# A graph and attention layer on one core: every k product ahead of every q product in the projections, counts begun three products earlier, a denser track of edge maxima

## The chip, the cores and the metric

One core of a Trainium2 chip runs the whole program. A core has five engines, each with its own in-order stream of instructions: TensorE (PE; its weight loads are shown apart as PEld), VectorE (DVE), ScalarE (ACT), GpSimd (POOL) and SyncE (SP), which here only issues DMAs. They meet through semaphores. The metric is the time of one execution on the device in microseconds, and a lower one is better. A difference under about 0.3% (5 us here) can't be told from no change by these measurements.

## The reference, cut to what matters

`xn` is the layer norm of `x` (1250 nodes, 768 columns). Three branches follow.

```python
# graph: three layers of graph attention over 21250 edges (+ loops), 4 heads of 192
h = (x1 @ W).reshape(N, H, C)
e = leaky_relu(as_n[src] + ad_n[dst], 0.2)
m = segment_max(e, dst);  p = exp(e - m[dst]);  s = segment_sum(p, dst)
out = segment_sum((p / s[dst])[:, :, None] * h[src], dst)
# mix: linear attention with random features, 12 heads of 64, 256 features
dash = (d ** -0.25 * data) @ proj.T          # for q and for k
diag = sum(data * data) * 0.5 * d ** -0.5
q' = ratio * (exp(dash - diag - max over the features of the row) + EPS)
k' = ratio * (exp(dash - diag - max over ALL heads, rows, features) + EPS)
out = q' (k'^T v) / (q' sum k');  mix = out @ w_proj.T + b_proj
x = x + relu(concat(graph layers) @ W_out + b_out) + mix
x = x + switch_ffn(layer_norm(x))            # 8 experts, top 1, capacity 195
```

The maximum of the k features runs over all twelve heads. So no k feature can be formed before every k projection and its `dash` product exist. The q maximum is one per row.

## The kernel before, in words

The nodes lie in NT = 10 tiles of 128 rows (98 in the last). The graph is not gathered edge by edge: indirect DMAs on POOL (`place`, L2093) scatter-add the edges into three tables of 1250x1250 counts in DRAM. Each tile of them is read back (`tab_in`), added on DVE and cast on ACT (`count`), turned on PE (`count_turn`), and made into `absent` on DVE, 0 where there is an edge and -3e38 where there is none (L1440). With `absent` in place, `edge_max` (L1452) is one DVE instruction per head and tile that takes the maximum of `as + absent` over a row: 12 heads x 10 tiles = 120. After the 40 of a layer, `shifts` forms exp's shifts on DVE, turns them (L1474) and writes them to DRAM; `head_in` reads them back as broadcast rows (`shift_b`). Then come 120 items of attention, each half a head by two tiles: `edge_z` (DVE, L1489 twice), `edge_exp` (ACT, L1882 twice), `weigh` (DVE, L1498) and `gather` (PE, 20 matmuls of L1047 into banks 0 to 2). `evict` and `finish` empty a half head.

Beside it runs the mix. The projections are 2 x 6 blocks n of 128 columns (a pair of heads each), by three chunks c of rows (512, 512, 226): 36 products m = 3n + c. A product (`qk`, PE, 18 matmuls) is squared and scaled on ACT, split into high and low parts on DVE (`qk_split`, L1387), its norms are matmuls (`norms`, L993, then DVE L1397), and a finished block is stored (`qk_store`, L2197). For a k block, ten `k_top` steps (three 512-column matmuls on PE, and DVE L1405, 0.69 us) take the maximum of each tile. Before the change even blocks are k and odd blocks q of the same pair, and the `k_top` of a k block are laid between the products of the q block behind it. After the last product come `top_max`, `top_turn` and `top_spread`, which make the one maximum. Then per pair of heads: ten `dash` for k with `k_exp` and `k_sum`, ten `dash` for q with `q_exp` (DVE L1521 and L1526, ACT L1921), `q_turn`, `q_feat`, `q_out` (L1101) and `divide` (L1536), and three steps of drain: 23 steps. Last come the output products of three of the row blocks (`row_block`: `row_in`, `row_turn` L1116, `row_split`, `row_mm`, `row_add`); in them the weights of the next block are loaded and split (`out_load`, `out_split` L1541). `expert_setup` prepares the routing once the graph's rows are out: POOL waits for their DMA, writes tables of indices, and DVE converts them (L1584 to L1588).

What stands where is set by one list, `ORDER`, that every engine runs through and of which it executes its own part. `whole_order` weaves generators into it. A `None` ends a step. The projections and then the mix advance one step at a time; a product is two steps. The graph's track advances beside them by rates: a rate of 0.75 yields an `edge_max` in three steps of four. `done` carries marks from one track to the other: `scattered` lets the counts begin, `projected` ends the first track's first part, `edges` is set after the last `edge_max`. The steps are numbered through here: the projections are steps 70 to 143 in both kernels.

## Time and profile before

| | us |
|---|---|
| median of 3 runs | 1726.52 |
| lowest, highest | 1725.98, 1729.97 |
| the profiled execution | 1718.87 |
| its span, first to last instruction | 1717.1 |

The profiled execution is itself 7.65 us below the median, and 1.8 us of it lies outside the span. A difference worked out on the trace is therefore taken off the median, not the trace's own time. PE is busy 91% of the span, DVE 66%, ACT 40%. To read such a profile for this change, one goes from the shares by engine to the busy time in stretches, and there asks which engine another one waits for.

### The profile page before, as it was taken

The page shows a single profiled execution, that of the slowest core. Times are in us where ns is not written, and L with a number is a line of the kernel's source. Part 1 is how long each engine was busy: PE and PEld are TensorE (multiplying, and loading weights), DVE is VectorE, ACT ScalarE, POOL GpSimd, SP SyncE. Part 2 cuts the span into 40 slices and gives each one's busy share as a digit, 9 for nine tenths or more (in the row PEclk, how much of TensorE's full clock was granted, in tenths as well). Part 3 has the DMA queues.
Part 4 walks back from the last instruction along what each step waited for, and adds up shares of the span by engine and source line. Part 5 has one row for each costly group of instructions (what it writes and reads, how often), then busy time and mean ns, then how long its engine had stood idle before and what let it go on. Part 6 is the DMA issues. An engine that isn't in the chain of part 4 may idle for free.

```text
span 1717.1 us, 24932 instructions
## 1 busy us (share of the span) xinstructions
PE 1565.3 (91%) x9666; PEld 1192.4 (69%) x9731; DVE 1129.8 (66%) x2573; ACT 681.6 (40%) x1359; POOL 410.1 (24%) x251
## 2 busy tenths in 40 slices
PE   3979999999989789999999979999999999986987
PEld 2556666555655467888888868888888966656664
DVE  6677664114466978797878789767975643885223
ACT  3421001122233467777777754434643431441110
POOL 3788888888400000000000000000000000002331
PEclk9999999999999979999999999999999999996999
DMA  9335545454652223234233044334530133645941
GB/s 353 84 67 118 119 78 118 68 94 65 191 183 87 91 78 135 72 99 131 63 101 95 27 153 134 129 129 151 164 125 29 60 114 135 231 180 211 321 146 50
DMA packets 194504, 213.66 MB, mean 124 GB/s; under 512 B 80975, under 2 KB 149213, under 8 KB 194386
## 3 DMA queue, kind: packets, MB, share of 16 engines
q1 hardware_dynamic: 117762, 187.01, 33.0%
q0 software_dynamic: 75760, 22.70, 8.4%
q10 hardware_dynamic: 864, 2.36, 0.4%
q8 instruction: 77, 1.26, 0.3%
q14 instruction: 41, 0.34, 0.1%
HBM read 144.74 MB, written 68.40 MB: 124 GB/s over the span
## 4 chain that ended last, share of the span: by engine, by line
PE 72%; DVE 17%; ACT 4%; issue 3%; DMA 2%; SPq 1%; POOLq 0%; POOL 0%; ACTq 0%; DVEq 0%
PE bank L1047 19%; PE bank L892 12%; PE bank L893 12%; PE bank L891 12%; PE bank L1217 4%; DVE junk L1452 3%; PE bank L1205 3%; PE bank L1101 3%; PE bank L1073 2%; DVE eb L1498 1%; DVE eb L1489 1%; PE bank L1116 1%; DVE q_max L1521 1%; PE bank L1086 1%; PE bank L993 1%
## 5 line engine op out<-in xcount | busy, mean ns | idle before, releaser
L1047 PE MATMUL bank<-hb,eb 128*128 128x193 f32 (+3 forms) x2400 | 419.9, 332 | 24.7 <-DVE eb L1498 14.0
L1047 PEld LDWEIGHTS bank<-hb,eb 128*128 128x128 f32 (+3 forms) x2400 | 400.3, 190 | 38.3 <-DVE eb L1498 17.1
L2093 POOL DMA_INDIRECT table<-amount,place x170 | 345.1, 2030 | 71.5 <-issue 49.5
L2099 POOL IOTA iota8i<- 128x8 int32 x1 | 0.1, 139 | 934.6 <-DMA node_rows<-node 934.6
L1489 DVE SCALAR_TENSOR_TENSOR eb<-shift_b,as_low,shift_b 128x640 f32<-128x640 f32 (+1 forms) x240 | 196.3, 859 | 7.8 <-DMA shift_b<-shift_rows 7.8
L1882 ACT ACTIVATE eb<-eb,asd 128x640 f32<-128x640 f32 (+1 forms) x240 | 182.0, 814 | 45.9 <-DVE eb L1489 45.9
L1498 DVE SCALAR_TENSOR_TENSOR eb<-eb,count 128x1280 f32<-128x1280 f32 (+1 forms) x120 | 174.4, 1454 | 12.4 <-ACT eb L1882 12.4
L1452 DVE CUSTOM_DVE_ANT_0 junk<-ab,absent 128x1250 bf16<-128x1250 f32 x120 | 174.4, 1453 | 1.0
L891 PE MATMUL bank<-wg_hi,x1T_hi 128*128 128x384 bf16 (+3 forms) x360 | 117.9, 328 | 0.6 <-DVE x1T_lo L1319 0.6
L893 PE MATMUL bank<-wg_hi,x1T_lo 128*128 128x384 bf16 (+3 forms) x360 | 117.9, 327 | 0.0
L892 PE MATMUL bank<-wg_lo,x1T_hi 128*128 128x384 bf16 (+3 forms) x360 | 117.8, 327 | 0.0
L891 PE MATMUL bank<-w_o_hi,aT_hi 128*128 128x384 bf16 (+1 forms) x360 | 117.4, 326 | 0.0
L893 PE MATMUL bank<-w_o_hi,aT_lo 128*128 128x384 bf16 (+1 forms) x360 | 117.3, 326 | 0.0
L892 PE MATMUL bank<-w_o_lo,aT_hi 128*128 128x384 bf16 (+1 forms) x360 | 117.3, 326 | 0.0
L892 PE MATMUL bank<-xnT_lo,wq_hi 128*128 128x512 bf16 (+1 forms) x211 | 72.0, 341 | 3.4 <-DVE wq_lo L1295 2.8
L893 PE MATMUL bank<-xnT_hi,wq_lo 128*128 128x512 bf16 (+1 forms) x215 | 73.4, 341 | 0.3
L1754 DVE TENSOR_TENSOR orow<-bank,b2r 105x384 f32<-105x384 f32 (+1 forms) x32 | 17.8, 556 | 84.5 <-PE bank L1217 76.1
L1333 DVE TENSOR_TENSOR h_row<-bank,bgr 128x384 f32<-128x384 f32 (+1 forms) x60 | 32.5, 555 | 62.1 <-PE bank L893 58.8
L1921 ACT ACTIVATE ef<-bank,q_shift 128x256 f32<-128x256 f32 (+1 forms) x120 | 50.3, 472 | 56.9 <-DVE q_shift L1526 56.9
L891 PE MATMUL bank<-xnT_hi,wq_hi 128*128 128x512 bf16 (+1 forms) x207 | 70.2, 339 | 0.2
L1828 ACT ACTIVATE wg_hi<-stage 128x776 bf16<-128x776 f32 x18 | 15.3, 850 | 132.9 <-DVE stage L1309 118.6
L1921 ACT ACTIVATE ef<-bank,k_shift 128x256 f32<-128x256 f32 (+1 forms) x120 | 49.9, 468 | 37.9 <-PE bank L893 37.6
(288 smaller groups left out, 2944.1 us busy)
## 6 DMA issues: line engine op xcount, KB each, us to landing
w<-in_w SPq DMA_DIRECT2D x16, 1152.0 KB, 20.1
shift_b<-shift_rows SPq DMA_DIRECT2D x24, 625.0 KB, 5.9
h_rows<-h_row SPq DMA_DIRECT2D x27, 388.0 KB
hb<-h_rows SPq DMA_DIRECT2D x12, 873.0 KB
ar<-node_rows SPq DMA_DIRECT2D x27, 384.0 KB
table<-zero POOLq DMA_DIRECT2D x3, 3054.0 KB, 21.1
tab<-table SPq DMA_DIRECT2D x27, 312.5 KB, 3.4
qk_rows<-qk_row SPq DMA_DIRECT2D x12, 625.0 KB
```

Source lines behind the costliest of these rows:

```text
L891: T.matmul(out_ap, lhs[0], rhs[0], start=first, stop=False, skip_group_check=skip)
L892: T.matmul(out_ap, lhs[0], rhs[1], start=False, stop=False, skip_group_check=skip)
L893: return T.matmul(out_ap, lhs[1], rhs[0], start=False, stop=last, skip_group_check=skip)
L1047: ins = T.matmul(bank[w // 2][0:M, c0:c0 + GC + 1], p[0:K, u, w * P:w * P + M], hv[0:K, t, 0:GC + 1], start=opens and u == 0 and w % 2 == ...
L1101: ins = T.matmul(ov[0:R, u, hh, :], qf[q % 4][:, hh * MT + m, 0:R], context[:, m, hh, :], start=u == 0 and hh == 0 and m == 0, stop=m == M ...
L1217: ins = T.matmul(bank[4 + i % 4][0:r1 - r0, 0:HROWS], hT[e % 2][:, f, r0:r1], w2s[e % WEIGHT_SETS][:, f, cs], start=f == 0, stop=f == KF - 1)
L1452: V.tensor_tensor_reduce(out=junk[0:R, :], in0=ab[lh % 2][0:R, :], in1=absent[0:R, t, :], scale=1.0, scalar=-BIG, op0=ALU.add, op1=ALU.max ...
L1489: ins = V.scalar_tensor_tensor(eb[i % EDGE_BUFFERS][:, u, 0:w], low, as_low[:, t, lh:lh + 1], high, ALU.add, ALU.max)
L1498: V.scalar_tensor_tensor(e, e, 1.0, count[:, 2 * pair:2 * pair + 2, ns], ALU.min, ALU.mult).then_inc(sem["edge_w"], 1)
L1882: ins = A.activation(e[:, u, 0:w], e[:, u, 0:w], ACT.Exp, bias=asd[:, t, 8 * l + hh:8 * l + hh + 1])
L1921: ins = A.activation(ef[g % 4][0:R, hh, :], bank[3 + g % 2][0:R, hh * FEATS:(hh + 1) * FEATS], ACT.Exp, bias=bias)
L2093: G.indirect_dma_start(tables[i], bass.IndirectOffsetOnAxis(place[:, c:c + 1], axis=0), amount16[:, c:c + 1], None, compute_op=ALU.add).th ...
```

## The change: what it does

- The blocks n = 0 to 5 are now all k, n = 6 to 11 all q (`w_from`, `norms`, `qk_store`, and L1866's wait, follow that). `k_top` of block n - 1 runs in blocks 1 to 6, so that they end in block 6 and not in block 11.
- `top_max`, `top_turn`, `top_spread` move from behind the last product to steps 117, 119 and 121. `pair_in(0)`, the loads of the mix's first pair, moves from step 99 to 117.
- `COUNTS_AT` goes from 17 to 14: the counts begin at step 98, not 104, in the fifth k block. Their turn on PE stands two steps later behind the count (3 for 2 in the track of rate 0.5).
- The rates of `edge_max` go from 0.75 to 1.0 in the projections and from 0.6 to 0.8 beside the mix; the 1.1 behind `projected` stays. By the end of the projections (step 143) 18 `edge_max` stand in the order, before 10. The last one stands at step 266, before 308.
- The attention waits for a mark `first` and has no empty steps. `shifts(0)` moves from step 172 to 164, `head_in(0)` from 174 to 166, the first `edge_z` from 178 to 166, the last `gather` from 422 to 410. The mix's own steps move up by two (its first `dash` from 147 to 145).

No instruction's shape or count changes.

```diff
@@ -65,8 +65,8 @@
 SLOT_TILES = 2 * EXPERTS
 NOWHERE = 4096.0
 
-COUNTS_AT = 17
-COUNT_RATE, EARLY_EDGE_RATE, FIRST_EDGE_RATE, EDGE_RATE, ATTENTION_RATE = 0.5, 0.75, 1.1, 0.6, 0.5
+COUNTS_AT = 14
+COUNT_RATE, EARLY_EDGE_RATE, FIRST_EDGE_RATE, EDGE_RATE, ATTENTION_RATE = 0.5, 1.0, 1.1, 0.8, 0.5
 
 
 def rows(t):
@@ -246,9 +246,9 @@
                 yield "qk_split", m - 1
             if part == 0 and c == 0 and n + 1 < 2 * PAIRS:
                 yield "w_split", 30 + n + 1
-            if n % 2 and 2 * c + part:
+            if 1 <= n <= PAIRS and 2 * c + part:
                 for t in range(4 * c + 2 * part - 2, 4 * c + 2 * part):
-                    yield "k_top", NT * (n // 2) + t
+                    yield "k_top", NT * (n - 1) + t
             if part == 0:
                 yield None
 
@@ -259,16 +259,14 @@
     def keep(m):
         if m % NC == NC - 1:
             yield "qk_store", m // NC
-        if m == NC * 4:
+        if m == NC * (PAIRS + 1):
             yield "pair_in", 0
+        for i, name in enumerate(("top_max", "top_turn", "top_spread")):
+            if m == NC * (PAIRS + 1) + i:
+                yield name, 0
 
     yield from in_step([(2, lambda m: [("norms", m)]), (0, product), (1, last_split), (2, keep)],
                        NC * 2 * PAIRS)
-    yield "top_max", 0
-    yield None
-    yield "top_turn", 0
-    yield None
-    yield "top_spread", 0
     done.add("projected")
     yield None
 
@@ -277,7 +275,7 @@
     while "scattered" not in done:
         yield None
     yield "ab_in", 0
-    yield from paced((in_step([(2, lambda t: [("count_turn", t), ("absent", t)]), (1, lambda t: [("count", t)]),
+    yield from paced((in_step([(3, lambda t: [("count_turn", t), ("absent", t)]), (1, lambda t: [("count", t)]),
                                (0, lambda t: [("tab_in", t)])], NT), COUNT_RATE))
     yield from spread(edge_layer(0), lambda: FIRST_EDGE_RATE if "projected" in done else EARLY_EDGE_RATE)
     while "projected" not in done:
@@ -320,8 +318,8 @@
         return []
 
     yield "head_in", 0
-    yield None
-    yield None
+    while "first" not in done:
+        yield None
     yield from in_step([(5, of_half("finish")), (5, mark), (4, of_half("evict")), (0, edge_z),
                         (1, lambda i: [("edge_exp", i)]), (2, lambda i: [("weigh", i)]), (3, lambda i: [("gather", i)])],
                        LH * ITEMS)
@@ -339,6 +337,8 @@
 
     def features(n):
         pair, kind, t = order[n]
+        if n == 2 * NT + 1:
+            done.add("first")
         if kind == "k" and t == 5 and pair + 1 < PAIRS:
             yield "pair_in", pair + 1
         if kind:
@@ -819,7 +819,7 @@
                 k = j - 24
                 return wT_qkv[k * 128:(k + 1) * 128, 2 * D:3 * D]
             n = j - 30
-            c = (1 - n % 2) * D + (n // 2) * 128
+            c = int(n < PAIRS) * D + n % PAIRS * 128
             return wT_qkv[:, c:c + 128].rearrange("(k p) c -> p k c", p=128)
 
         def w_views(j):
@@ -1002,9 +1002,9 @@
             def k_top(i):
                 pair, t = divmod(i, NT)
                 pe.wait_ge("feats_lo", 1)
-                pe.wait_ge("qk_lo", NC * (2 * pair + 1))
+                pe.wait_ge("qk_lo", NC * (pair + 1))
                 pe.wait_ge("k_max", i - 1)
-                dash_into(4 + i % 2, qk_out[0], t).then_inc(sem["top_mm"], 1)
+                dash_into(4 + i % 2, qk_out[pair % 2], t).then_inc(sem["top_mm"], 1)
 
             def top_turn(_):
                 pe.wait_ge("top_v", 1)
@@ -1389,7 +1389,7 @@
 
             def norms(m):
                 n = m // NC
-                which, pair = 1 - n % 2, n // 2
+                which, pair = int(n < PAIRS), n % PAIRS
                 c0, c1 = chunk(m)
                 t0 = c0 // P
                 ve.wait_ge("norm_mm", m + 1)
@@ -1416,7 +1416,7 @@
                 ve.wait_ge("top_pe", 2)
                 V.tensor_copy(top[0:P, 2:3], bank[5][0:P, P:P + 1]).then_inc(sem["top_v"], 1)
                 ve.wait_ge("top_v", 3)
-                ve.wait_ge("diag_in", 2 * PAIRS * NC)
+                ve.wait_ge("diag_in", PAIRS * NC)
                 V.tensor_scalar(k_shift[:, :, :], diag[:, 1, :, :], top[0:P, 2:3], -1.0, ALU.add,
                                 ALU.mult).then_inc(sem["top_v"], 1)
 
@@ -1861,8 +1861,8 @@
                 se.wait_ge("norm_mm", m - 2)
                 A.activation(sq[m % 3][:, 0:c1 - c0], b, ACT.Square).then_inc(sem["qk_square"], 1)
                 se.wait_ge(f"qk_out{n % 2}", 16 * (n // 2))
-                if n % 2 == 0:
-                    se.wait_ge("top_mm", NT * (n // 2))
+                if n >= 2:
+                    se.wait_ge("top_mm", NT * min(n - 1, PAIRS))
                 A.activation(qk_out[n % 2][:, 0, c0:c1], b, ACT.Copy, scale=NORM).then_inc(sem["qk_hi"], 1)
 
             def count_(t):
@@ -2194,7 +2194,7 @@
 
             def qk_store(n):
                 sy.wait_ge("qk_lo", NC * (n + 1))
-                S.dma_start(qk_rows[1 - n % 2, n // 2], qk_out[n % 2][:, :, :]).then_inc(sem[f"qk_out{n % 2}"], 16)
+                S.dma_start(qk_rows[int(n < PAIRS), n % PAIRS], qk_out[n % 2][:, :, :]).then_inc(sem[f"qk_out{n % 2}"], 16)
 
             def tab_in(t):
                 R = rows(t)
@@ -2259,7 +2259,7 @@
                 else:
                     sy.wait_ge("qk_mm", NC * 2 * PAIRS)
                 for j in range(2):
-                    sy.wait_ge(f"qk_out{j}", 16 * (PAIRS if pair else 1))
+                    sy.wait_ge(f"qk_out{j}", 16 * (PAIRS if pair else PAIRS // 2 + 1 - j))
                     sy.wait_ge(f"v_out{j}", 16 * HALF)
                 if pair >= 2:
                     sy.wait_ge("dash_mm", dash_of(pair - 2, "k", NT - 1) + 1)
```

DVE at the seam of graph layer 0: `shifts(0)` is the five rows that end in STREAM_TRANSPOSE, `edge_z` is L1489, `edge_max` the pair of L1452 rows. Before:

```order
L1469 TENSOR_TENSOR shift<-asd,ms 128x10x4
L1470 SCALAR_TENSOR_TENSOR shift<-asd,ms 128x10x4
L1474 STREAM_TRANSPOSE shift_t<-shift 128x320
L1452 ISA junk,m_col<-ab_248,absent 128x1250
L1452 ISA m_col 128x1
L1452 ISA junk,m_col<-ab_248,absent 128x1250
L1452 ISA m_col 128x1
L1489 SCALAR_TENSOR_TENSOR eb_153<-shift_b_251,as_low,shift_b_250 128x640 x2
```

and after:

```order
L1469 TENSOR_TENSOR shift<-asd,ms 128x10x4
L1470 SCALAR_TENSOR_TENSOR shift<-asd,ms 128x10x4
L1474 STREAM_TRANSPOSE shift_t<-shift 128x320
L1521 TENSOR_REDUCE q_max<-bank 98x2
L1526 SCALAR_TENSOR_TENSOR q_shift<-q_max,diag 98x2
L1536 RECIPROCAL inv<-bank 128x4
L1489 SCALAR_TENSOR_TENSOR eb_153<-shift_b_251,as_low,shift_b_250 128x640 x2
L1452 ISA junk,m_col<-ab_248,absent 128x1250
L1452 ISA m_col 128x1
L1536 RECIPROCAL inv<-bank 128x4
```

The first `edge_z` now stands ahead of the `divide` (the last L1536) that frees the mix's output bank; before, both last `divide` of the pair stood ahead of it.

PE behind the last `gather` (L1047): L1116 are the turns of the rows of output block 2, L891 its first product. Before:

```order
L1047 MATMUL bank<-hb_224,eb_156 98x193
L1116 MATMUL bank<-ident,ar_105 128x128 x6
L1047 MATMUL bank<-hb_224,eb_157 128x193 x8
L1047 MATMUL bank<-hb_224,eb_157 98x193 x2
L1116 MATMUL bank<-ident,ar_106 128x128 x6
L891 MATMUL bank<-w_o_hi,aT_hi 128x384
```

and after:

```order
L1047 MATMUL bank<-hb_224,eb_157 128x193 x8
L1047 MATMUL bank<-hb_224,eb_157 98x193 x2
L1116 MATMUL bank<-ident,ar_105 128x128 x6
L1116 MATMUL bank<-ident,ar_106 128x128 x6
L891 MATMUL bank<-w_o_hi,aT_hi 128x384
```

The first turn stood ahead of the last `gather` and now stands behind it, so nothing of PE's is left between the turns and the product.

DVE at the same place: `finish(23)` is L1507 and L1511, `expert_setup` L1584 to L1588, `row_split` of a row tile L1561, `out_split` L1541. Before:

```order
L1541 TENSOR_TENSOR w_o_lo<-st_0_242,w_o_hi 128x768
L1561 SCALAR_TENSOR_TENSOR aT_lo<-bank,aT_hi 128x384 x2
L1541 TENSOR_TENSOR w_o_lo<-st_1_243,w_o_hi 128x768
L1507 TENSOR_SCALAR rinv<-node_160 128x4
L1507 TENSOR_SCALAR rinv<-node_160 98x1
L1511 RECIPROCAL rinv<-rinv 128x4
L1511 RECIPROCAL rinv<-rinv 98x1
L1561 SCALAR_TENSOR_TENSOR aT_lo<-bank,aT_hi 128x384 x2
L1580 TENSOR_TENSOR wacc<-bank,wacc 128x384
L1584 MEMSET stats_91 128x160
```

and after:

```order
L1511 RECIPROCAL rinv<-rinv 128x4
L1511 RECIPROCAL rinv<-rinv 98x1
L1584 MEMSET stats_91 128x160
L1585 MEMSET pm 128x80
L1586 TENSOR_SCALAR iota_82<-iota8i 128x8
L1587 CAST idx<-idx_i 128x20
L1588 CAST iota_row<-iota_i 128x105
L1541 TENSOR_TENSOR w_o_lo<-st_0_242,w_o_hi 128x768
L1561 SCALAR_TENSOR_TENSOR aT_lo<-bank,aT_hi 128x384 x2
```

`expert_setup` stood behind the split of the block's first two row tiles and now stands ahead of both.

## Rows read from the trace of the kernel before

**Rows 1.** The page: busy time by engine, then three groups (count, busy us, mean ns).
```profile
PE 1565.3 (91%) x9666; PEld 1192.4 (69%) x9731; DVE 1129.8 (66%) x2573; ACT 681.6 (40%) x1359; POOL 410.1 (24%) x251
...
L1489 DVE SCALAR_TENSOR_TENSOR eb<-shift_b,as_low,shift_b 128x640 f32<-128x640 f32 (+1 forms) x240 | 196.3, 859 | 7.8 <-DMA shift_b<-shift_rows 7.8
...
L1498 DVE SCALAR_TENSOR_TENSOR eb<-eb,count 128x1280 f32<-128x1280 f32 (+1 forms) x120 | 174.4, 1454 | 12.4 <-ACT eb L1882 12.4
L1452 DVE CUSTOM_DVE_ANT_0 junk<-ab,absent 128x1250 bf16<-128x1250 f32 x120 | 174.4, 1453 | 1.0
```

**Rows 2.** Stretches: length, busy PE, PEld, DVE, ACT, POOL, granted clock, DMA.
```profile
371.00:572.00 201.00, 185.36 (x1146) 112.83 (x1167) 114.40 (x232) 53.39 (x94) 68.00 (x34) 0.98 0.46 122
572.00:620.00 48.00, 35.44 (x227) 24.64 (x230) 46.69 (x82) 31.29 (x69) 0.00 (x0) 0.93 0.28 95
621.00:641.00 20.00, 19.45 (x78) 15.62 (x81) 9.74 (x20) 10.45 (x25) 0.00 (x0) 0.50 0.29 83
660.00:982.00 322.00, 310.26 (x2061) 282.55 (x2091) 267.03 (x411) 237.91 (x519) 0.00 (x0) 1.00 0.25 80
982.00:1060.00 78.00, 62.56 (x361) 58.61 (x360) 71.69 (x97) 41.49 (x80) 0.00 (x0) 0.93 0.41 131
1060.00:1379.00 319.00, 315.58 (x1962) 271.64 (x1960) 227.46 (x306) 138.31 (x249) 0.00 (x0) 0.99 0.35 115
```

**Rows 3.** SP's timeline: start, length. Blocks 5 to 7 of the projections are stored.
```profile
461.15 0.32 SPq L2197 DMA_DIRECT2D qk_rows<-qk_row  x1
...
480.00 0.32 SPq L2197 DMA_DIRECT2D qk_rows<-qk_row  x1
...
505.69 0.32 SPq L2197 DMA_DIRECT2D qk_rows<-qk_row  x1
```

**Rows 4.** PE's timeline (idle before, releaser in brackets): last norms, first `dash` recorded.
```profile
571.79 0.53 PE L993 MATMUL bank<-halves,sq 128*128 128x2 f32 x4 [2.23 <-DVE diag L1397]
...
576.79 0.63 PE L892 MATMUL bank<-feats_lo,k_first 128*128 128x512 bf16 x1 [0.33 <-issue]
```

**Rows 5.** DVE's timeline: pair 0's last `q_exp`, `shifts(0)`'s turn, and the first `edge_z`.
```profile
618.22 0.69 DVE L1521 TENSOR_REDUCE q_max<-bank 98x2 f32<-98x512 f32 x1
...
631.57 0.51 DVE L1474 STREAM_TRANSPOSE shift_t<-shift 128x320 f32<-128x320 f32 x1
...
642.78 1.68 DVE L1489 SCALAR_TENSOR_TENSOR eb<-shift_b,as_low,shift_b 128x640 f32<-128x640 f32 x2 [7.84 <-DMA shift_b<-shift_rows]
```

**Rows 6.** PE's timeline: the first `k_sum` of pair 1.
```profile
630.44 0.88 PE L1073 MATMUL bank<-vs,ef 128*128 128x65 f32 x3
```

**Rows 7.** DVE's timeline: first `q_exp` of pairs 0, 1 and 5.
```profile
596.97 0.69 DVE L1521 TENSOR_REDUCE q_max<-bank 128x2 f32<-128x512 f32 x1
...
650.25 0.69 DVE L1521 TENSOR_REDUCE q_max<-bank 128x2 f32<-128x512 f32 x1 [1.32 <-PE bank L893]
...
949.72 0.69 DVE L1521 TENSOR_REDUCE q_max<-bank 128x2 f32<-128x512 f32 x1 [3.28 <-PE bank L893]
```

**Rows 8.** DVE's timeline: `weigh` of items 51 and 63 (steps 284 and 308).
```profile
990.99 1.48 DVE L1498 SCALAR_TENSOR_TENSOR eb<-eb,count 128x1280 f32<-128x1280 f32 x1
...
1057.26 1.48 DVE L1498 SCALAR_TENSOR_TENSOR eb<-eb,count 128x1280 f32<-128x1280 f32 x1
```

**Rows 9.** The timeline of all engines from the last `gather` on.
```profile
1375.60 3.45 PE L1047 MATMUL bank<-hb,eb 128*128 128x193 f32 x20
...
1379.55 0.33 PE L891 MATMUL bank<-w_o_hi,aT_hi 128*128 128x384 bf16 x1
...
1381.57 1.84 ACT L1906 ACTIVATE node<-node,rinv 128x192 f32<-128x192 f32 x5 [1.42 <-DVE rinv L1511]
...
1383.43 0.37 SPq L2251 DMA_DIRECT2D node_rows<-node  x1
...
1387.17 0.19 DVE L1584 MEMSET stats<- 128x160 f32 x1 [1.87 <-POOL iota_i L2102]
...
1389.01 1.00 DVE L1561 SCALAR_TENSOR_TENSOR aT_lo<-bank,aT_hi 128x384 bf16<-128x384 f32 x2
```

## The prediction, made before the changed kernel had run

> **What bounds the kernel now.** I read the page first, then the busy times of the stretches that the change touches, then the timelines at their borders. PE is busy 1565 of 1717 us [rows 1], so what an edit of order can win is PE's idle time and the time that it spends at half clock. PE's work is the same in both kernels. Up to the end of the last `gather` both have done the same of it (but one turn), so I carry a clock from border to border until there, and then price what follows. The stretches [rows 2] show where idle time lies. In the projections PE is busy 185 of 201 us. In the mix's first pair (572 to 620) PE is busy 35 of 48 and DVE 46.7: DVE holds it, with `edge_max` of 1.5 us a piece (1.45 [rows 1] and the read of its result). [...] From 660 to 982 PE is busy 96% and DVE 83%. From 982 to 1060 DVE is busy 92% and PE 80%: only attention items run there, with `edge_max`, and DVE holds it again. From 1060 to the last `gather` PE is 99% busy. So the sizes to win are some 15 us (projections), 12 (pair 0), 15 (982 to 1060), and part of the half clock. DVE's `edge_max` is the load that the change moves to the front.
>
> **Projections (steps 70 to 143).** A block with counts alone takes 18.9 us, one with counts and `k_top` 25.7 (461.15, 480.00, 505.69 [rows 3]). Before, counts meet no `k_top`, then `k_top`, then none; after, they meet them in blocks 5 and 6 and not in 7 and 8. The difference of 6.8 between the kinds is what ten `k_top` take on PE and DVE wherever they stand, so the sum of the blocks stays. The later turn of the counts lifts a wait of PE for ACT's cast; I estimate it at up to 2 us. Against it, 18 and not 10 `edge_max` stand beside the last blocks: in their 18 steps DVE has 18 x 1.5 = 27 us and some 7 of splits and norms, PE some 30. That is up to 4 us too much. I take 0, with -3 and +4 as ends. The counts can't read before the scatter is over in either kernel; SP reaches that wait a little earlier, and what is queued behind it (a weight load two blocks ahead, a store) is not due. The `top` steps cost PE and DVE a fraction of a microsecond each amid the products.
>
> **Seam.** From the last norms to the first recorded `dash` matmul are 5.0 us (571.79, 576.79 [rows 4]), the three `top` steps queued behind `edge_max`. After, only norms (0.5) and their copy on DVE, behind one `edge_max`, are left: 2 us. Gain 3 us (ends 1.5 and 5). The first `dash` is at 573.8.
>
> **Pair 0 and the wait for the shifts.** The rate there is 1.1 in both kernels, so DVE still holds it: the first `q_exp` moves from 597.0 to 594.3 [rows 7]. From there to the end of `shifts(0)` DVE has nine `q_exp` (6.6), nine `edge_max` (13.2, at 1.47) and the shifts (1.3): 615.4. In the trace the turn starts at 631.57, ends at 632.08, and the first `edge_z` starts at 642.78, having idled 7.84 for the broadcast rows [rows 5]: 10.7 us for a write and a read through DRAM, which SP issues at once in both kernels. Before, two `edge_max` and nothing that PE needs lay in this wait. After, the first `edge_z` stands two steps behind the shifts, blocks DVE until 615.4 + 10.7 = 626.1, and ahead of the `divide` that PE's last `q_out` of the pair waits for. Then come `edge_z` (1.7), `edge_max` (1.5), `divide` (0.1), and ACT (0.8): PE resumes at 630.2. It ran out of work at about 619.5, behind the last turn, one `q_out` and one `dash`. **This new wait costs PE some 10.7 us.** Behind it DVE still has two `edge_max`, an `edge_z` and the last `divide` (4.7, and ACT's 0.8) ahead of pair 1's first `k_sum`: 635.0, where it was 630.4 [rows 6]. So the lead of 2.7 us has turned into 4.6 behind, at the same point of the mix. What is gained is that the attention runs twelve steps earlier.
>
> **Pair 1 to pair 5 (the costliest guess).** From 630.4 to the first `q_exp` of pair 1 are 19.8 us [rows 6, 7]; 11 of these at half clock cost 5.4, so PE's work is 14.4. After, four `gather` (3.3 each: 1375.60 to 1379.55 less the turn of 0.65 [rows 9]) stand in it: 14.4 + 13.2, and I leave 3.4 us for half clock: 31.0, and 666. From there to pair 5's first `q_exp` are 299.5 us now, 92 steps. DVE is busy 83% of that, 248 us, and gets 0.2 x 1.5 us a step more: 276, or 92%. PE's share is 289 us. Both are near full, in one lockstep with two banks for `dash`, so some of it will not fit: I take 2 us for each of four pairs, 8 in all. The ends are 0 (all of it falls into DVE's idle time) and 25 (nearly the whole 27.6). So pair 5's first `q_exp` is at 974, now 949.7.
>
> **Pair 5 to the last `gather`.** To item 51 are 41.3 us now [rows 7, 8]; without `edge_max` PE's own work is left, about 38: 1012. The 12 items from 51 to 63 (990.99, 1057.26 [rows 8]) take 66.3 us, and DVE's part without `edge_max` is 12 x 3.09 (196.3 and 174.4 over 120 items [rows 1]) = 37 and six weight splits of 0.95. I add 3 for weights that come late: 46, and 1058. **This gains 20 us.** From 1057.3 to the end of the last `gather` (1378.9 [rows 9]) PE has no slack [rows 2], 321.6 us; five `gather` fewer are left: 305. The last `gather` ends at 1363, 16 us earlier.
>
> **Behind the last `gather`.** Now PE goes straight on (1379.55 [rows 9]), 0.65 behind the last `gather`. In the new order all matmuls that lay between are done, and the output block's first product needs a `row_split` on DVE that stands behind `expert_setup`. Its chain, from the last `gather`: `evict` 0.5, reciprocals 0.6, ACT's scaling 1.8 (1381.57 to 1383.41), store issued; to `expert_setup` on DVE 3.7 (1383.43 to 1387.17), through DMA and POOL; its five instructions 0.5, a weight split 0.9, the row split 1.0 [rows 9]: about 9.3 us. **PE idles 8.6 us that it did not before.** The half clock that follows such a gap takes at most a couple of us more: I add 1.7. That gives back 10.3. The ends are 4 and 14. From there on both orders are alike, and PE-bound.
>
> **The sum.** -16 + 10.3 = -5.7, on the trace 1717.1 to about 1711. The profiled execution is below the median, so I take it off that: 1726.5 - 6 = **1720.5**.
>
> [...] The row of 621 to 641 shows a clock that fell to half while PE's gaps were of 1 to 2 us, and stayed there with PE 97% busy on the mix's narrow matmuls. [...] The sum leaves 3.4 and 1.7 us for it.
>
> **Rivals.**
> - *The gaps are milder (1709).* The `gather` beside pair 1 bring the clock back at once, the wide order of the mix holds the 92% without loss. Then 8 and 3.4 us are saved: -17. For it: from 660 on the clock is 1.00. Against: PE already idles 4% there with DVE at 83%.
> - *DVE holds the mix (slower, 1738).* With a dense track the pairs' period goes up by 2 us in my sum; each more microsecond costs 4. It is 0 for the kernel at 3.4 us a pair, and slower beyond 0.3% from 4.7 us on. At 6.3 us (25 in all), -6 + 17 = +11. For it: pair 0, where DVE's load is over PE's, runs at DVE's pace with PE 74% busy. Against: summed over a pair DVE's load is still 13 us under PE's.
> - *The wait for the shifts and the tail eat it all (1727).* The lead of 16 is halved by late weights and a longer half clock: no change.
> - *The change doesn't do what it says:* the order shows that all of it is in place; 0.
>
> **Chances.** The forecast's own case 0.46 (1715 to 1726; a bit over half of it under 1721.3, the bound of faster by 0.3%), milder gaps 0.25, DVE holding 0.19 (a fifth of it within 0.3%), nothing left 0.10. Faster 0.49, within 0.3% 0.34, slower 0.17. For 8 in 10 the range runs from 1704 (milder gaps, and the projections' -3 and the seam's 2) to 1737.
>
> **What will show it.** Right: the projections end within 4 us of 571; the first `dash` follows within 3 us; DVE idles near 10 us ahead of the first `edge_z` and PE about as long at the last `q_out` of pair 0; the pairs' period is 76 to 77 us, not 74.6; the twelve items beside the weight loads take under 50 us; PE idles 8 to 9 us behind the last `gather`. Wrong: a period of 78 and more, or a PE that finds work in either gap.

## The result: 8.6 us slower, where 6 us less were forecast

| | before | after |
|---|---|---|
| median, us | 1726.52 (5 runs) | 1735.14 (5 runs) |
| lowest, highest | 1725.48, 1730.93 | 1733.17, 1737.04 |
| the profiled execution | 1718.87 | 1734.36 |
| its span | 1717.1 | 1732.6 |

The ratio is 1.0048, with a 95% interval of 1.0033 to 1.0063: slower, by more than the 0.3% that a measurement can tell. The forecast was 1720.5, 6 us less. Its range (1704 to 1737) holds the result, but the direction is the other one, and that the range reaches so far up is luck: its upper end came from a rival (DVE holds the mix) that the trace refutes. A second trace of the kernel before (the run before_again below) has a span of 1725.8. So the two first traces differ by 15.5 us, but the medians by 8.6: the trace of before was a quick one.

**Busy time first**, as in [rows 1]: the page after, engines and the three groups.

```profile
PE 1569.8 (91%) x9664; PEld 1195.5 (69%) x9731; DVE 1129.9 (65%) x2573; ACT 680.9 (39%) x1359; POOL 409.6 (24%) x251
...
L1489 DVE SCALAR_TENSOR_TENSOR eb<-shift_b,as_low,shift_b 128x640 f32<-128x640 f32 (+1 forms) x240 | 196.4, 860 | 9.8 <-DMA shift_b<-shift_rows 9.8
...
L1498 DVE SCALAR_TENSOR_TENSOR eb<-eb,count 128x1280 f32<-128x1280 f32 (+1 forms) x120 | 174.6, 1455 | 5.5 <-ACT eb L1882 5.5
L1452 DVE CUSTOM_DVE_ANT_0 junk<-ab,absent 128x1250 bf16<-128x1250 f32 x120 | 174.6, 1455 | 1.4
```

No engine does more than before: PE is busy 1569.8 us for 1565.3 with the same instructions, and the surplus goes with more time at half clock (the mean granted clock of the span is 0.964, before 0.973 and 0.966). The time is in the order: in waits.

**By stretch.** The windows after: pair 0, the half clock, pairs 1 to 5, the twelve items beside the weight loads (`weigh` 56 to 68; the same place of the mix as 51 to 63 before), from there to the last `gather`, and the rest. Columns as in [rows 2].

```profile
574.50:620.00 45.50, 37.80 (x219) 27.55 (x222) 41.78 (x72) 29.58 (x64) 0.00 (x0) 0.85 0.25 86
625.00:648.00 23.00, 14.05 (x55) 10.63 (x57) 16.48 (x24) 10.74 (x24) 0.00 (x0) 0.50 0.68 217
660.00:1004.00 344.00, 328.70 (x2183) 298.38 (x2215) 295.99 (x460) 253.96 (x552) 0.00 (x0) 1.00 0.26 83
1013.03:1066.15 53.12, 45.83 (x270) 44.27 (x271) 42.75 (x55) 33.23 (x61) 0.00 (x0) 0.97 0.49 157
1066.15:1380.70 314.55, 305.74 (x1890) 260.64 (x1889) 211.22 (x281) 128.77 (x232) 0.00 (x0) 0.98 0.33 109
1380.70:1732.60 351.90, 296.86 (x1757) 210.23 (x1755) 173.19 (x452) 80.01 (x171) 48.61 (x54) 0.92 0.52 171
```

The last three of them in the second trace of before:

```profile
998.83:1064.95 66.12, 51.48 (x285) 48.94 (x286) 62.13 (x85) 33.43 (x61) 0.00 (x0) 0.92 0.45 140
1064.95:1386.70 321.75, 318.34 (x1981) 273.43 (x1980) 230.31 (x308) 140.57 (x253) 0.00 (x0) 0.99 0.36 117
1386.70:1725.80 339.10, 291.41 (x1751) 207.17 (x1749) 170.85 (x449) 77.95 (x168) 48.45 (x54) 0.94 0.53 173
```

The twelve items [rows 8] took 13 us less (66.1 to 53.1). The way to the last `gather` took only 7 less (321.8 to 314.6), though five `gather` fewer, of 3.3 us each, were left. What follows took 12.8 more (339.1 to 351.9).

**The three waits.** In PE's timeline after, three idle times stand out; the first and the third have no partner before, the second has a shorter one. The first is the one of pair 0, at the `q_out` that stands behind the first `edge_z` (DVE's row first; it answers [rows 5], PE's last row [rows 6]):

```profile
631.52 1.68 DVE L1489 SCALAR_TENSOR_TENSOR eb<-shift_b,as_low,shift_b 128x640 f32<-128x640 f32 x2 [9.78 <-DMA shift_b<-shift_rows]
```
```profile
635.69 3.31 PE L1101 MATMUL bank<-context,qf 128*128 128x65 f32 x16 [8.62 <-ACT att L1958]
...
640.38 1.94 PE L1073 MATMUL bank<-vs,ef 128*128 128x65 f32 x8
```

The second is behind the mix's output products, where only `gather` is left for PE while the output weights 6 to 11 are loaded and split. PE first:

```profile
1228.66 1.66 PE L1047 MATMUL bank<-hb,eb 128*128 128x193 f32 x4 [5.21 <-DVE eb L1498]
```

The longest wait for `eb` at this place before:

```profile
1206.83 1.64 PE L1047 MATMUL bank<-hb,eb 128*128 128x193 f32 x7 [2.42 <-DVE eb L1498]
```

DVE, ACT and SP after:

```profile
1224.72 0.96 DVE L1541 TENSOR_TENSOR w_o_lo<-st,w_o_hi 128x768 bf16<-128x768 f32 x1 [6.54 <-ACT w_o_hi L1970]
```
```profile
1223.84 0.84 ACT L1970 ACTIVATE w_o_hi<-st 128x768 bf16<-128x768 f32 x1 [8.28 <-DMA st<-in_W_out]
```
```profile
1195.73 13.57 SPq L2298 DMA_DIRECT2D st<-in_W_out  x5
1211.24 0.38 SPq L2251 DMA_DIRECT2D node_rows<-node  x1
1211.66 0.49 SPq L2253 DMA_DIRECT2D node_rows<-node  x1
1212.20 1.40 SPq L2239 DMA_DIRECT2D shift_b<-shift_rows  x2
...
1214.12 2.37 SPq L2244 DMA_DIRECT2D hb<-h_rows  x1
1216.53 0.46 SPq L2298 DMA_DIRECT2D st<-in_W_out  x1
```

A weight split (ACT and DVE) stands ahead of a `weigh`; it waits for its load, and that load stands on SP behind a node store and the loads of the next head. The place in the queue is the smaller part of it. The load is issued at 1216.53, and its reader starts 7.3 us later, while the 16 DMA engines are full:

```profile
1217.00:1224.00 7.00, 5.22 (x20) 4.92 (x20) 1.18 (x1) 0.16 (x1) 0.00 (x0) 0.76 1.05 363
```

Before, a node store stood at this place too, but no loads of a head, and the same load took 3.1 us (issued 1203.00, read at 1206.09). The third is behind the last `gather` and answers [rows 9]:

```profile
1387.51 0.19 DVE L1584 MEMSET stats<- 128x160 f32 x1 [5.90 <-POOL iota_i L2102]
```
```profile
1389.57 1.51 PE L1116 MATMUL bank<-ident,ar 128*128 128x128 f32 x6 [8.19 <-DVE aT_lo L1561]
```

Together 22 us, of which 3.4 us of waits for `eb` (1.00 and 2.42) stood in the second place before, too. The experiments ask two things: are these the loss, and what is the rest of the change worth without them?

### The profile page after: what moved, and what is told of

Read it like the earlier page. It is cut to its first block, busy times and chain, and to the rows that moved or that the text cites. A ratio compares the mean times of both kernels' runs of the same rounds, so it can differ in the third digit from the quotient of the medians.

```text
span 1732.6 us, 24931 instructions
## 1 busy us (share of the span) xinstructions
PE 1569.8 (91%) x9664; PEld 1195.5 (69%) x9731; DVE 1129.9 (65%) x2573; ACT 680.9 (39%) x1359; POOL 409.6 (24%) x251
## 4 chain that ended last, share of the span: by engine, by line
PE 73%; DVE 15%; ACT 4%; issue 3%; DMA 3%; SPq 1%; POOL 0%; POOLq 0%; ACTq 0%; DVEq 0%
PE bank L1047 18%; PE bank L892 13%; PE bank L893 13%; PE bank L891 12%; PE bank L1217 4%; PE bank L1205 3%; PE bank L1073 3%; DVE junk L1452 2%; PE bank L1101 2%; PE bank L1116 1%; DVE q_max L1521 1%; DVE eb L1498 1%; DVE eb L1489 1%; PE bank L993 1%; PE bank L901 1%
## 5 line engine op out<-in xcount | busy, mean ns | idle before, releaser
L1047 PE MATMUL bank<-hb,eb 128*128 128x193 f32 (+3 forms) x2400 | 417.5, 330 | 25.4 <-DVE eb L1498 12.8
L1047 PEld LDWEIGHTS bank<-hb,eb 128*128 128x128 f32 (+3 forms) x2400 | 398.2, 189 | 38.8 <-DVE eb L1498 17.4
L1489 DVE SCALAR_TENSOR_TENSOR eb<-shift_b,as_low,shift_b 128x640 f32<-128x640 f32 (+1 forms) x240 | 196.4, 860 | 9.8 <-DMA shift_b<-shift_rows 9.8
L1452 DVE CUSTOM_DVE_ANT_0 junk<-ab,absent 128x1250 bf16<-128x1250 f32 x120 | 174.6, 1455 | 1.4
L891 PE MATMUL bank<-w_o_hi,aT_hi 128*128 128x384 bf16 (+1 forms) x360 | 119.7, 332 | 0.0
L891 PE MATMUL bank<-wg_hi,x1T_hi 128*128 128x384 bf16 (+3 forms) x360 | 117.9, 328 | 0.6 <-DVE x1T_lo L1319 0.6
L891 PE MATMUL bank<-xnT_hi,wq_hi 128*128 128x512 bf16 (+1 forms) x205 | 70.1, 342 | 0.1
L1101 PEld LDWEIGHTS bank<-context,qf 128*128 128x128 f32 (+1 forms) x480 | 58.3, 195 | 13.4 <-ACT att L1958 10.4
```

Of the source, the lines that this page charges most:

```text
L891: T.matmul(out_ap, lhs[0], rhs[0], start=first, stop=False, skip_group_check=skip)
L1047: ins = T.matmul(bank[w // 2][0:M, c0:c0 + GC + 1], p[0:K, u, w * P:w * P + M], hv[0:K, t, 0:GC + 1], start=opens and u == 0 and w % 2 == ...
L1101: ins = T.matmul(ov[0:R, u, hh, :], qf[q % 4][:, hh * MT + m, 0:R], context[:, m, hh, :], start=u == 0 and hh == 0 and m == 0, stop=m == M ...
L1452: V.tensor_tensor_reduce(out=junk[0:R, :], in0=ab[lh % 2][0:R, :], in1=absent[0:R, t, :], scale=1.0, scalar=-BIG, op0=ALU.add, op1=ALU.max ...
L1489: ins = V.scalar_tensor_tensor(eb[i % EDGE_BUFFERS][:, u, 0:w], low, as_low[:, t, lh:lh + 1], high, ALU.add, ALU.max)
```

## The experiments

Each kernel is the changed one unless said otherwise, and each computes the whole reference. Most edits use one helper behind `ORDER`, which takes steps out and puts them behind another one:

```python
def moved(order, steps, behind):
    rest = [s for s in order if s not in steps]
    at_ = rest.index(behind) + 1
    return rest[:at_] + list(steps) + rest[at_:]
```

Each ratio is against the kernel before as timed beside that run; its median there was 1726.5 to 1728.3 us.

| run | median, us | ratio to before | 95% interval |
|---|---|---|---|
| after | 1735.14 | 1.0048 | 1.0033 to 1.0063 |
| e_first | 1728.32 | 1.0000 | 0.9982 to 1.0018 |
| e_load | 1731.57 | 1.0018 | 0.9999 to 1.0037 |
| e_tail | 1728.82 | 1.0005 | 0.9987 to 1.0022 |
| e_all | 1718.40 | 0.9949 | 0.9932 to 0.9967 |
| before_again | 1727.23 | 0.9992 | 0.9972 to 1.0011 |
| k_only | 1726.38 | 0.9996 | 0.9977 to 1.0016 |
| mix_only | 1751.37 | 1.0145 | 1.0117 to 1.0174 |
| e_spread | 1707.42 | 0.9881 | 0.9854 to 0.9908 |
| before_spread | 1723.61 | 0.9972 | 0.9960 to 0.9984 |
| k_spread | 1723.41 | 0.9969 | 0.9953 to 0.9986 |
| e_loads | 1712.27 | 0.9898 | 0.9875 to 0.9921 |
| spread06 | 1724.00 | 0.9977 | 0.9960 to 0.9993 |

### The three waits, one by one and together

**e_first.**

```diff
+ORDER = moved(ORDER, [("edge_z", 0), ("edge_z", 1), ("edge_exp", 0)], ("divide", 0, 4))
```

> The changed kernel with the first three steps of the attention's pipeline (edge_z of items 0 and 1, edge_exp of item 0) moved behind divide(0, 4) of pair 0, so that PE doesn't stand at the first edge_z for the vector and scalar engines while k_sum and q products wait behind it. Nothing is left out. Theory 1: the 8.62 us in which PE waits for att at 635.69 go, at least in part (3 to 8 us), pair 1's first k_sum comes at 632 to 637 and not at 640.4, and the time is 1727 to 1732, 1.000 to 1.003 of the kernel before. Rival A (the attention's start is late whatever stands ahead, and its items are missed behind): k_sum(1,0) earlier, but the last gather again at 1380 and the time within 2 us of 1735. Rival B (the order itself, half clock from 577 to 591): k_sum(1,0) at 638 or later, since the k products and q maxima at half clock set it.

Measured: 1.0000, 0.0048 less than the change, some 8 us. PE's timeline there:

```profile
624.81 0.70 PE L1095 MATMUL bank<-ident,ef 98*128 98x98 f32 x4 [1.37 <-ACT ef L1930]
625.63 3.68 PE L1110 MATMUL bank<-context,qf 128*128 128x65 f32 x16
...
635.23 1.94 PE L1082 MATMUL bank<-vs,ef 128*128 128x65 f32 x8
```

The `q_out` follows without a gap, and pair 1's first `k_sum` comes at 635.2 and not at 640.4. Theory 1 holds. Not all of it reached the end in this trace: the second wait grew.

```profile
1223.23 1.01 PE L1056 MATMUL bank<-hb,eb 128*128 128x193 f32 x2 [7.21 <-DVE eb L1507]
```

7.21 us and not 5.21. That an earlier PE waits longer for the same load is my reading; no run isolates it.

**e_load.**

```diff
+ORDER = moved(ORDER, [("finish", 17), ("head_in", 10)], ("out_load", 11))
```

> The changed kernel with two steps moved: finish(17) and head_in(10) stand behind out_load(11) and not amid out_load(6) to out_load(11), so that on SP's queue the node store, shift_b and hb no longer stand ahead of the loads that out_split(11) waits for. Nothing is left out. Theory 1: the 5.21 us in which PE waits for the vector engine's weighing (eb, L1498) at 1228.66 go, with the half clock behind it (6.8 us at half clock, some 3 us of it lost): time 1727 to 1731, 1.000 to 1.003 of the kernel before; the last gather ends 5 to 8 us earlier than 1380.6, at 1373 to 1376. Rival A (the vector engine is full there, so the wait comes back a few gathers later): last gather at 1379 to 1381 and time within 2 us of 1735. Rival B (the order itself): the same as rival A in time.

Measured: 1.0018, about 5 us less than the change; the two intervals together allow 1 to 9. But my cause was only half right:

```profile
1225.37 1.11 PE L1056 MATMUL bank<-hb,eb 128*128 128x193 f32 x4 [4.36 <-DVE eb L1507]
```
```profile
1221.43 0.96 DVE L1550 TENSOR_TENSOR w_o_lo<-st,w_o_hi 128x768 bf16<-128x768 f32 x1 [2.64 <-ACT w_o_hi L1979]
```

With nothing between the loads on SP, a wait of 4.36 us is still there. The six loads share two `st` buffers and follow one another within some 20 us; each split waits for its own load. The `gather` before, which waited 1.28 and 2.32 us after the change, waits 0.91 us here. From `weigh` 68 to the last `gather` are 309.0 us, 5.6 less than after the change. The last `gather` itself ended at 1380.4, against the 1373 to 1376 expected: this trace came to `weigh` 68 5.5 us later (1071.6 for 1066.15), in part by a half clock of 20.5 us and not 13.6 behind the seam.

**e_tail.**

```diff
+ORDER = moved(ORDER, [("row_in", 20)], ("row_add", 37))
+ORDER = moved(ORDER, [("row_turn", 20), ("row_split", 20), ("row_in", 21)], ("gather", 118))
+ORDER = moved(ORDER, [("expert_setup", 0)], ("row_add", 41))
```

> The changed kernel with its last steps in another order: the input of the last row block, its turn and split, and the setup of the expert section stand behind the last gather and the last row additions, and not ahead of them, so that the vector engine's 5.90 us wait for iota_i at 1387.5 no longer stands ahead of aT_lo, for which PE waits 8.19 us at 1389.57. Nothing else is moved and nothing left out. Theory 1 (three relocated waits eat what the moved edge maxima gained; this is one of them): PE idles under 2 us between the last gather and row_mm(40), and the time falls by 6 to 9 us from the changed kernel's 1735, to 1726 to 1729, 1.000 to 1.002 of the kernel before. Rival A (behind the last gather the section waits for the vector engine in any order): the wait only shows behind another instruction, PE still idles 6 us or more, and the time stays within 2 us of 1735. Rival B (the loss lies in the k-first order itself, by the clock or by the mix): the gap may close, but the half clock of the last section eats it, and the time stays above 1731.

Measured: 1.0005, 7 us less than the change, as theory 1 had it. The window from the last `gather` to the end, 351.9 after:

```profile
1386.20:1730.00 343.80, 294.14 (x1751) 209.22 (x1749) 171.74 (x450) 78.95 (x170) 48.65 (x54) 0.93 0.52 174
```

8.1 us shorter. PE still waits once, 3.21 us for `aT_lo`, so not all of it is gone.

**e_all**, the three together.

> The three moves of the other runs together. Theory 1 (three separate waits on PE's path): the gains add, 6 to 9 and 4 to 7 and 3 to 8 us, so 1713 to 1721, 0.992 to 0.997 of the kernel before, and the changed kernel's other parts are worth their 8 to 12 us. Rival A (one engine, the vector engine, is behind all three, and a gap that closes opens again later): the gains don't add, and the time is 1725 or more. Rival B (the k-first order and its half clock cost it): 1728 or more.

Measured: 0.9949, faster than before. The single gains are 0.0048, 0.0030 and 0.0043, in sum 0.0121 (21 us); together they gave 0.0099 (17 us), the same within the intervals. So the three gains add, and both rivals fall: the loss sits in three places, each of which a step's position made, and not in one full engine or in the k-first order.

### The two halves of the change, and before once more

**before_again** is the kernel before, unchanged.

> The kernel before, unchanged, for a second trace of it: its first profiled execution lasted 1718.9 us against a median of 1726.5, and the changed kernel's 1734.4 against 1735.1. If the first trace was a quick one, this one is 3 to 10 us longer, and the stretches in which the surplus lies (last norms at 572.1, last gather's end at 1378.9, last section 338.2 us) tell which of the differences between the two traces belong to the run and not to the change. Theory 1 (the last section's +13.9 us are the order's): the last section takes 338 to 340 us again. Rival B (the last section varies by run with the clock): it takes 342 or more. Ratio to before 0.998 to 1.002.

Measured: 0.9992, and a span of 1725.8, 8.7 us over the first trace. The last section took 339.1 us (first trace 338.2), so theory 1 holds. 6 of the 8.7 us lie between the last norms and pair 0's first `q_exp`, where this trace was at half clock for 23.6 us and the first was at full clock from 580 on:

```profile
577.00:600.60 23.60, 19.98 (x73) 14.36 (x74) 22.78 (x36) 12.09 (x22) 0.00 (x0) 0.50 0.43 148
```

The first trace, for comparison:

```profile
573.00:580.00 7.00, 3.26 (x8) 1.31 (x9) 6.91 (x13) 2.06 (x3) 0.00 (x0) 0.51 0.92 308
580.00:597.00 17.00, 15.24 (x106) 11.23 (x108) 16.51 (x25) 14.29 (x29) 0.00 (x0) 1.00 0.29 95
```

**k_only**: the changed kernel with the counts, the rates and the attention's start as before.

```diff
-COUNTS_AT = 14
-COUNT_RATE, EARLY_EDGE_RATE, FIRST_EDGE_RATE, EDGE_RATE, ATTENTION_RATE = 0.5, 1.0, 1.1, 0.8, 0.5
+COUNTS_AT = 17
+COUNT_RATE, EARLY_EDGE_RATE, FIRST_EDGE_RATE, EDGE_RATE, ATTENTION_RATE = 0.5, 0.75, 1.1, 0.6, 0.5
...
-    yield from paced((in_step([(3, lambda t: [("count_turn", t), ("absent", t)]), (1, lambda t: [("count", t)]),
+    yield from paced((in_step([(2, lambda t: [("count_turn", t), ("absent", t)]), (1, lambda t: [("count", t)]),
...
-    while "first" not in done:
-        yield None
+    yield None
+    yield None
```

> The k-first half of the change alone: k projections ahead of q, early k maxima and the seam as in the changed kernel; counts' start, their lag, the rates of the edge maxima and the attention's start as before. Nothing is left out. Theory 1 (the waits that came with the moved mix cost it): the seam gains nothing or up to 3 us (in the changed kernel last norms to first q_exp took 25.2 us, before 24.9), no PE wait for att near 635, last section at 338 to 340 us, and the time is 0.997 to 1.001 of the kernel before, 1723 to 1729. Rival B (the k-first order costs it): 1.002 to 1.005, 1731 to 1736, and last norms to first q_exp over 26 us.

Measured: 0.9996, no difference. Rival B falls: the k-first order alone costs nothing. It gains nothing either: this trace is 8.1 us ahead of before_again at pair 0's first `q_exp` (598.3 for 606.4), but 3.3 us at the end of the twelve items (1061.6 for 1064.95), where PE now waits 7.33 us at once for the eviction of `node`.

**mix_only**: the kernel before with just these lines of the change (counts, rates, attention's start).

> The other half of the change alone: the kernel before with its interleaved projections, but counts begun four products ahead, their turns a step later, the two edge rates at 1.0 and 0.8, and the attention's start behind the second half of the first q products. Nothing is left out. Theory 1: it has the three waits (PE for att near 635, 6 to 10 us; for eb near 1225, 4 to 6; for aT_lo behind the last gather, 8), and the time is 1.003 to 1.007 of the kernel before, 1731 to 1738. Rival B (the k-first order is what costs): 0.998 to 1.002.

Measured: 1.0145, 24 us slower than before, and well beyond what my theory gave. The three waits are there (5.69 us at 649.72, 4.10 at 1243.61, 8.16 at 1404.35). The surplus is a fourth, in the projections:

```profile
467.03 0.61 PE L893 MATMUL bank<-feats_hi,qk_row 128*128 128x512 bf16 x1 [10.39 <-DVE kmax L1407]
```
```profile
461.42 0.81 DVE L1429 TENSOR_TENSOR count<-tab,tab 128x1250 uint16<-128x1250 uint16 x1 [9.54 <-DMA tab<-table]
```

DVE reaches the first count before the scattered tables are there. PE's next `k_top` waits behind it, and runs at half clock at first (granted clock 0.50; a record of the 512-column matmul lasts 0.61 us there and 0.38 at full clock). The changed kernel's first count starts at 461.61, with no wait: by its order, 42 `k_top` stand ahead of the first count, in mix_only 22, and ten take 6.8 us [rows 3]. **So the k-first order is what makes the early counts possible**: with it the same lines cost 9 us and not 24.

### What the moved maxima are worth once nothing waits

**e_spread**: e_first's and e_tail's moves, and the loads and splits of the weights spread out.

```diff
+for j in range(6, 12):
+    ORDER = moved(ORDER, [("out_load", j)], ("gather", 75 + 2 * (j - 6)))
+    ORDER = moved(ORDER, [("out_split", j)], ("gather", 78 + 2 * (j - 6)))
```

> The changed kernel with the attention's first steps behind divide(0, 4) and the last steps behind the last gather as in e_first and e_tail, and, in place of e_load's move, the loads and splits of the output weights 6 to 11 spread over the gathers 75 to 88, one every two, and not one behind another at gathers 88 to 92. e_load showed that SP's queue was not the whole of the wait: 4.36 us of the 5.21 came back two gathers earlier, behind a vector engine that waited 2.01 and 2.64 us for w_o_hi, each of which waits for its load of st. Theory (the two st buffers, loaded one behind another within 20 us, hold the weighing): spread out, no wait for eb over 1.5 us stands between 1190 and 1240, the mix's second half is 5 to 7 us shorter than in the run of all three moves (967.5 to 1369.8 there), and the time is 1710 to 1714, 0.990 to 0.993 of the kernel before. Rival (the vector engine is full there, whoever feeds it): waits of the same 5 to 6 us in sum, elsewhere, and 1716 to 1721.

Measured: 0.9881, 1707.4 us, faster than both kernels and than the 1710 to 1714 expected (4 executions). From the twelve items to the last `gather`:

```profile
1061.22:1363.33 302.11, 302.11 (x1896) 257.88 (x1895) 211.56 (x283) 129.37 (x234) 0.00 (x0) 1.00 0.35 114
```

302.1 us, all of it busy at full clock, where the changed kernel took 314.6 and before took 321.8. The rival (a full DVE) falls: loads in quick succession, beside a head's loads, were the cause.

**before_spread** and **k_spread**: the same spreading, five gathers earlier, in the kernel before and in k_only.

```diff
+for j in range(6, 12):
+    ORDER = moved(ORDER, [("out_load", j)], ("gather", 70 + 2 * (j - 6)))
+    ORDER = moved(ORDER, [("out_split", j)], ("gather", 73 + 2 * (j - 6)))
```

> The kernel before with the loads and splits of the output weights 6 to 11 spread over its gathers 70 to 83, one every two, as e_spread did it for the changed kernel (1707.4 us, 0.988, there together with the other two moves). It tells how much of that belongs to this spreading, and so what the change itself is worth. Before, the stretch has waits of 1.00 and 2.42 us for eb at 1200.9 and 1206.8 and a dip to half clock of 3.4 us. If only these waits go: 2 to 5 us, 0.997 to 0.999, 1723 to 1726. If the spreading also shortens the mix elsewhere (e_spread's second half of the mix was 6.8 us shorter than in the run of all three moves, whose waits there were 5.4 us): 5 to 8 us, 0.995 to 0.997.

> The k-first half alone with the same spreading. k_only was 0.9996 of the kernel before. If the two add: like before_spread less 0 to 1 us, 1722 to 1726. Against it stands e_spread with 1707.4: what is left between the two, 14 to 18 us, would be the worth of the moved edge maxima once nothing waits behind them. If k_spread comes to 1712 or less, most of the gain is the spreading's and the moved maxima are worth little.

Measured: 0.9972 and 0.9969. Spreading is worth 5 us by itself, and again the k-first order adds nothing. What remains between these and e_spread (0.9881) or e_loads (0.9898) is 0.007 to 0.009, 12 to 16 us: that is what the rest of the change is worth, with the waits that it made taken away. Whether the moves of e_first and e_tail would also speed up the kernel before was not run; its last section (340.5 us in before_spread) is shorter than e_spread's (346.4), so the traces show nothing to win there.

**e_loads**, one more wait attacked.

```diff
+ORDER = moved(ORDER, [("out_load", 18)], ("gather", 110))
+ORDER = moved(ORDER, [("out_load", 19)], ("gather", 112))
+ORDER = moved(ORDER, [("row_turn", 21), ("row_split", 21), ("out_split", 18), ("out_load", 20)], ("evict", 23))
```

> e_spread with one place more set right: out_load(18) and out_load(19) stand behind gathers 110 and 112, and the turn and split of row 21 ahead of the splits of the output weights 18 and 19, so that the 3.59 us in which PE waits for aT_lo at 1373.4 (the scalar engine there waits 3.99 us for a load of st that stands behind the node store on SP's queue) go. Expected: no wait for aT_lo over 1 us between the last gather and row_mm(42), last section 339 to 342 us against 346.5, time 1702 to 1706, 0.985 to 0.988 of the kernel before. Rival (the wait moves to the next row's split, since the loads come two at a time): 1706 to 1709.

Measured: 0.9898, 1712.3 us, no better than e_spread and above both of the ranges that I gave. In kind it is the rival: the wait has changed its name, for the rows of the next tile:

```profile
1375.98 0.77 PE L1134 MATMUL bank<-ident,ar 128*128 128x128 f32 x5 [3.50 <-DMA ar<-node_rows]
```

**spread06**: e_loads with the rate of the second and third graph layers as before.

```diff
-COUNT_RATE, EARLY_EDGE_RATE, FIRST_EDGE_RATE, EDGE_RATE, ATTENTION_RATE = 0.5, 1.0, 1.1, 0.8, 0.5
+COUNT_RATE, EARLY_EDGE_RATE, FIRST_EDGE_RATE, EDGE_RATE, ATTENTION_RATE = 0.5, 1.0, 1.1, 0.6, 0.5
```

> e_loads with the second layer's edge maxima at the old rate, 0.6 and not 0.8 a step; counts' start, the first layer's rates and the attention's start stay as in the changed kernel. The last edge maximum then stands behind q_exp of pair 5 and not at the end of pair 4. Theory (the gain comes from a vector engine that is free of the maxima when the gathers are bare, behind the last pair at 1004 to 1066): waits for eb come back there, 6 to 12 us, and the time is 1708 to 1716, 0.990 to 0.994. Rival (the early start of the first layer's maxima does it, the rate is idle): within 2 us of e_loads.

Measured: 0.9977, 12 us over e_loads, more than I expected. From pair 5's first `q_exp` to just behind `weigh` 67, e_loads first and spread06 second:

```profile
970.00:1061.00 91.00, 82.13 (x512) 77.81 (x511) 65.47 (x95) 61.07 (x127) 0.00 (x0) 0.96 0.36 113
```
```profile
969.10:1073.00 103.90, 88.25 (x521) 82.12 (x520) 91.13 (x136) 60.48 (x126) 0.00 (x0) 0.93 0.34 105
```

DVE has 25.7 us more to do there, PE waits 15.7 us and not 8.9, and is at half clock for longer. Spread06 keeps the early counts, the first layer's rates and the attention's early start, and yet is as fast as k_spread (0.9969). So without the rate of 0.8 the change gains nothing, and what begins earlier gains nothing by itself. Whether the rate alone would do it, without the early start, was not run.

## Why the prediction was wrong

Two terms of the sum failed. The twelve items were to gain 20 us and gained 13.2. And the stretch from there to the last `gather` was to take 305 us and took 314.6: the shifted order beside the weight loads, which the sum had at nothing, made 8.8 us of waits where 3.4 were, and 10.2 us at half clock where 3.4 were. By the prediction's own terms, on the trace (each forecast border against the measured one):

- **Projections, 0: right in size.** The last norms are at 574.2, in the second trace of before at 575.1. The reason was incomplete. I said that the counts can't read before the scatter is over "in either kernel" and left it; mix_only shows that this is worth 10 us of PE's time, and that the twenty `k_top` more that stand ahead of the first count (13.6 us at 6.8 for ten) cover it.
- **Seam, 3 us: a little too low.** From the last norms to pair 0's first `q_exp` are 24.9 us in the first trace of before, 31.0 in the second, 25.2 after and 21.6 in k_only. Two more traces of the old order have about 31 (before_spread, mix_only), so against the usual 31 the change gains 5 to 6, though k_only's median shows that this need not reach the end; on the quick trace it showed nothing, and I had the first `q_exp` at 594.3, where it came at 599.7.
- **Pair 0 and the wait for the shifts: right.** DVE idles 9.78 us (I had 10.7 from the turn to the `edge_z`; 631.52 less 620.87 is 10.65), PE 8.62 (I had 10.7), and `k_sum` of pair 1 comes at 640.4 for 635.0, all of the difference from the seam. e_first shows it to be worth 8 us. Before, an `edge_max` at this place takes 1.48 us from its start to the next one's (619.12 to 620.60), with the 0.09 us of its result's read in it.
- **Pairs 1 to 5: right.** The first `q_exp` of pairs 1 and 5, which I had at 666 and 974, answer [rows 7]:

```profile
667.86 0.69 DVE L1521 TENSOR_REDUCE q_max<-bank 128x2 f32<-128x512 f32 x1 [1.79 <-PE bank L893]
...
972.40 0.69 DVE L1521 TENSOR_REDUCE q_max<-bank 128x2 f32<-128x512 f32 x1 [3.17 <-PE bank L893]
```

  The period is 304.5 / 4 = 76.1 us. The rival "DVE holds the mix" falls. The 3.4 us for half clock behind `k_sum` were my estimate: after, PE was at half from 640.4 to 648.7, which by the same halving costs some 4.
- **The twelve items, "this gains 20 us": wrong, 13.2.** I took DVE's work without the maxima (37, and 5.7 for the splits; measured 42.8 together), added 3 us, and had 46. DVE's work was right, but relieved of the maxima DVE no longer bounds: PE alone is busy 45.8 us there, and 7.3 us of waits, for evictions and weighing most of all, stay. What I left out is one window: before, PE was busy 51.5 of these 66.1 us (second trace, above), so its idle time was 14.6 us, and the dips to half clock (0.92 on the mean) held some 5 more. A gain of 20 needed all of it to vanish. My own list of what there was to win had 15 us and some half clock for this place.
- **To the last `gather`, 305 us: wrong, 314.6.** I took "PE has no slack" from before and carried it over. The order of the steps beside the weight loads had changed: before, `finish(16)` stood amid them, and now `finish(17)` with the loads of a head, `head_in(10)`. PE's waits for `eb` were 8.8 us (3.4 before), with 10.2 us at half clock for 3.4. e_spread's 302.1 shows that the 305 were there to be had. I had costed this shift at nothing, and had named SP's queue only where it did no harm. This term and the one before it are 17 of the 21 us by which the trace's end was missed.
- **Behind the last `gather`, 10.3 us: right in kind, a little low.** PE waited 8.19 us (8.6 forecast), with the chain of POOL's tables and `expert_setup` in it; the 1.7 us for half clock were my estimate, and PE was at half from the gap's end at 1389.57 to 1392.8, which costs 1.6; the last section took 12.8 us more than in the second trace of before. e_tail gets 8 back.
- **From the trace to the median.** I took the difference off the median, 1726.5. The trace of before was 7.65 below its median and the one of after 0.8 below, so the trace's miss of 21 us became 15 in the median. The second trace says where its 8.7 us lie: most of them at the seam, by the clock.

In time the nearest of my rivals is "DVE holds the mix" (1738), but its mechanism did not occur: the period was 76.1 us. In mechanism the nearest is "the wait for the shifts and the tail eat it all" (1727). It had late weights as well, but only as something that halves the lead, and so ended at no change. Without the waits the change is worth 12 to 16 us. That this is near the 16 us that my sum had up to the last `gather` is chance, for those 16 had the wait of 10.7 us in them.

**The half clock and the gaps.** In e_first, which has no gap of 8.6 us in pair 0, the clock is at half all the same:

```profile
625.10:645.50 20.40, 19.38 (x76) 14.54 (x76) 14.86 (x23) 14.21 (x33) 0.00 (x0) 0.50 0.88 288
```

PE is 95% busy at a granted clock of 0.50. Just ahead of it, at full clock, PE was busy 3.00 of 5.10 us, in pieces, and no gap was over 1.37 us:

```profile
620.00:625.10 5.10, 3.00 (x25) 2.60 (x24) 4.93 (x13) 2.97 (x9) 0.00 (x0) 1.00 0.02 2
```

After the change the same dip, with the gap of 8.62 us in it, is 24 us long, and it too begins ahead of the gap (at 624.9; the gap begins at 627.1). So it isn't the long gap that brings the half clock here. Behind the last `gather`, where the gap of 8.19 us (1381.38 to 1389.57) is new, a dip of 6.8 us (1386.0 to 1392.8) comes with it, where both traces of before are at full clock (1.00). It begins inside the gap.

## What to carry to other kernels

Bound a gain by what the engine that sets the end can win in that stretch, its idle time and its time at half clock, and not by the load taken from its neighbour: in the twelve items that bound was 14.6 us and some 5, and relief of DVE won 13.2. A list of steps that is shifted against another gives the steps other neighbours in their queues: look at each place where loads with few buffers follow one another (here a new wait of 5.21 us), at the first read behind a write through DRAM (8.62), and at the last section (8.19), and price those before the gain. And where a change has several parts, try each part alone and all of them with the waits removed: here one half alone cost 24 us, the whole 9, and with the order put right in three places the same change became the fastest version, 1.2% under the kernel before.
